# Causal masks, activation table calls, the order of calls and the first head of a two-layer attention kernel

## The reference, cut to what matters

```python
xn = layer_norm(_layernorm(x), gamma_in)
q, k, v = heads(xn @ Wq) * 64 ** -0.5, heads(xn @ Wk), heads(xn @ Wv)
sim = einsum('bhid,bhjd->bhij', q, k)
sim = where(causal_mask, -max, sim)            # triu(ones, k=1)
attn = softmax(sim)
out = einsum('bhij,bhjd->bhid', attn, v)
adj = clip(attn + eye(n), 0, 1); deg = sum(adj, -1)
feats = v
for l in range(2):
    h = feats @ gnn_w[l] + gnn_b[l]
    feats = gelu(adj @ h / deg + feats)        # per head
out = out + feats @ lin_w + lin_b
y = x + _layernorm(layer_norm(out @ Wo, gamma_out))
# then two layers of local attention and feed-forward, a norm and a residual
```

## Time and profile before

| What | Value |
|---|---|
| Median of 3 runs | 1573.04 us (1572.93 to 1578.7) |
| Profiled execution | 1574.63 us |
| Its span, first to last instruction | 1572.8 us |
| Mean granted TensorE clock | 0.975 |
| Busy: TensorE, weight load, VectorE, ScalarE, POOL | 92%, 71%, 75%, 63%, 23% |
| First product of the maxima of head 0 | 34.88 us |
| First scores of head 0 | 47.65 us |

### The profile page before, as it was taken

The page is one execution under the profiler, slowest core; times in us unless marked ns, Lnnn a source line. Parts: engine busy times, 40 slices in busy tenths (PEclk is TensorE's granted clock), DMA queues, the critical chain, the costliest instruction groups (busy, mean ns, idle before and its releaser), DMA issues. The chain is left out here.

```text
span 1572.8 us, 29162 instructions
## 1 busy us (share of the span) xinstructions
PE 1441.3 (92%) x10194; PEld 1109.0 (71%) x10194; DVE 1181.4 (75%) x3237; ACT 995.3 (63%) x2307; POOL 367.7 (23%) x474
## 2 busy tenths in 40 slices
PE   4899999999999999999999999999788999999896
PEld 3577877778777787777777777777455666666663
DVE  4577777777777777777878777776787888888875
ACT  2366666666666666666666666666355877778573
POOL 2022222221122111222222222223222332222211
PEclk8899999999999999999999999999987999999998
DMA  6021111211112111121111121220300000100100
GB/s 172 14 51 32 28 28 29 43 39 28 28 31 48 32 28 28 31 44 35 28 28 28 38 45 28 58 48 1 91 21 11 21 21 21 25 18 21 28 12 20
DMA packets 41147, 54.36 MB, mean 35 GB/s; under 512 B 11774, under 2 KB 23978, under 8 KB 41002
## 3 DMA queue, kind: packets, MB, share of 16 engines
q1 hardware_dynamic: 41002, 52.51, 15.0%
HBM read 9.89 MB, written 1.05 MB: 7 GB/s over the span
## 5 line engine op out<-in xcount | busy, mean ns | idle before, releaser
L1098 ACT ACTIVATE t<-PS 128x512 f32<-128x512 f32 (+3 forms) x384 | 188.9, 492 | 148.4 <-PE PS L661 94.5
L1544 DVE TENSOR_REDUCE t<-PS 128x1 f32<-128x512 f32 (+3 forms) x384 | 210.7, 550 | 77.3 <-PE PS L634 54.4
L1561 DVE TENSOR_TENSOR t<-t 128x512 fp32r<-128x512 f32 (+3 forms) x384 | 211.5, 551 | 9.6 <-ACT t L1099 9.4
L1099 ACT ACTIVATE t<-PS 128x512 fp32r<-128x512 f32 (+3 forms) x384 | 188.6, 491 | 0.0
L713 PE MATMUL PS<-t 128*128 128x512 f32 (+3 forms) x384 | 150.1, 391 | 21.9 <-ACT t L1132 21.6
L632 PE MATMUL PS<-t 128*128 128x512 f32 (+3 forms) x384 | 140.8, 391 | 24.8 <-DMA t<-t 13.0
L1248 ACT ACTIVATE t<-PS,t 128x128 f32<-128x128 f32 x256 | 113.2, 463 | 67.7 <-DVE t L1804 67.7
L660 PE MATMUL PS<-t 128*128 128x512 f32 (+3 forms) x384 | 149.0, 388 | 2.7 <-DMA t<-t 2.2
L1408 POOL TENSOR_TENSOR t<-t 128x16 f32<-128x16 f32 x32 | 92.8, 2900 | 234.1 <-DVE t L1666 234.1
L678 PE MATMUL PS<-t 128*66 128x512 f32 (+3 forms) x384 | 138.8, 361 | 0.0
L661 PE MATMUL PS<-t 65*128 65x512 f32 (+3 forms) x384 | 133.7, 348 | 0.0
(11 more groups left out here) (189 smaller groups left out, 3872.5 us busy)
## 6 DMA issues: line engine op xcount, KB each, us to landing
t<-t SPq DMA_DIRECT2D x188, 128.0 KB, 2.3
t<-t SPq DMA_DIRECT2D x64, 256.0 KB, 3.4
t<-in_c_rot SPq DMA_DIRECT2D x4, 512.0 KB, 5.6
t<-in_L_ffn_wqkv SPq DMA_DIRECT2D x2, 768.0 KB, 7.6
t<-in_L_attn_Wv SPq DMA_DIRECT2D x2, 512.0 KB, 7.4
out<-t SPq DMA_DIRECT2D x4, 256.0 KB, 2.3
t<-in_L_ffn_w SPq DMA_DIRECT2D x2, 341.0 KB
t<-in_L_attn_x SPq DMA_DIRECT2D x2, 256.0 KB, 3.2
```

Of the source, the lines that this page charges most:

```text
L1098: e.activation(Es[:, k % NS, 0:n], b[:, 0:n], ACT.Exp).then_inc(a_es.up((t, k)), 1)
L1099: e.activation(Eh[:, o:o + n], b[:, 0:n], ACT.Exp).then_inc(a_eh.up((t, k)), 1)
L1544: e.tensor_reduce(n[:, c, ib:ib + 1], bank(k % 2)[:, 0:hi - lo], AX.X, ALU.max, negate=True).then_inc(d_max.up((t, k)), 1)
L1561: e.tensor_tensor(El[:, o:o + n], Es[:, k % NS, 0:n], f32(Eh[:, o:o + n]), ALU.subtract).then_inc(d_el.up((t, k)), 1)
```

## The change

- **Masks.** The mask products (lines 634 and 663) and `cmB` are gone. VectorE adds the mask in place in PSUM on 128x128, `causal` ahead of a maximum and `acausal` ahead of an exponential, with new signals `d_cm` and `d_sm`. ScalarE's `scores` waits for `d_sm` in the diagonal tiles.
- **Tables.** Before all else ScalarE takes the exponential of one column into `fsc`. In each turn `exp_table` stands after tile 4 of the scores, and `gelu_table` after tile 11, one column each.
- **Order.** The calls of the loop are put in another order on TensorE, VectorE, ScalarE and POOL. `widen_v` is split off `widen`; both stand at the end of POOL's turn.
- **Head 0.** POOL writes the weights of K and of Q twice side by side (`twins`, in the space of `El`), so that `head0` on TensorE gives K in both halves of bank 2 + c and Q in both halves of bank 4 + c. ScalarE and VectorE write `K1`, `K2`, `Q1` and `Q2` of head 0 from there, without `part(0)` and `double(0)`. The work ahead of the loop is interleaved with the maxima of head 0, `part(1)` and `double(1)` come ahead of the loads of WG, Wo and the second half of x, and `mrow(0)` behind them. The loads of `wqkv0`, the band, the shift and `gam_out` move into turn 4.

```diff
             def smax(t, k):
...
-                diag = c == ib // 4
-                m = e.matmul(bank(b)[:, 0:hi - lo], Q1[r][:, ib * P:(ib + 1) * P], K1[r][:, lo:hi], start=True, stop=not diag)
-                if diag:
-                    m = e.matmul(bank(b)[:, hi - lo - P:hi - lo], identB[:], cmB[:, 0, :], start=False, stop=True)
-                m.then_inc(p_max.up((t, k)), 1)
+                e.matmul(bank(b)[:, 0:hi - lo], Q1[r][:, ib * P:(ib + 1) * P], K1[r][:, lo:hi], start=True,
+                         stop=True).then_inc(p_max.up((t, k)), 1)
...
-                if diag:
-                    m = e.matmul(b[:, 0:P], identB[:], cmB[:, 1, :], start=False, stop=True)
...
+            def causal(t, k):
...
+                q.wait_ge(*p_max[t, k])
+                s = bank(k % 2)[:, o:o + P]
+                e.tensor_tensor(s, s, cm[:, 0, :], ALU.add).then_inc(d_cm.up((t, k)), 1)
...
+            def acausal(t, k):
...
+                q.wait_ge(*p_sc[t, k])
+                s = bank(2 + k % 2)[:, 0:P]
+                e.tensor_tensor(s, s, cm[:, 1, :], ALU.add).then_inc(d_sm.up((t, k)), 1)
...
             def scores(t, k):                      # ScalarE
...
-                q.wait_ge(*p_sc[t, k])
                 q.wait_ge(*(d_el[t, k - NS] if k >= NS else d_el[t - 1, k + NTL - NS]))
                 q.wait_ge(*p_hop[t - 1, k])
+                q.wait_ge(*(d_sm if jb >= 4 * c else p_sc)[t, k])
...
+            def gelu_table(t):
...
+                e.activation(fsc[:, 0:1], half[:, 0:1], ACT.Gelu)
...
+            def head0(c):                          # TensorE
+                q.wait_ge(*d_turn[c])
+                q.wait_ge(*w_wd[0])
+                sl = slice(c * 512, (c + 1) * 512)
+                for i in range(2):
+                    b = bank(2 + 2 * i + c)
+                    e.matmul(b, twins[:, i, 0, :], xh[:, sl], start=True, stop=False)
+                    e.matmul(b, twins[:, i, 1, :], xh[:, sl], start=False, stop=False)
+                    m = e.matmul(b, twins[:, i, 0, :], xl[:, sl], start=False, stop=True)
+                m.then_inc(p_proj.up((0, c)), 1)
...
+            def head0(c):                          # ScalarE
...
+                e.copy(K1[0][:, sl], bank(2 + c)).then_inc(a_k0.up(c), 1)
+                e.activation(Q1[0][:, sl], bank(4 + c), ACT.Copy, scale=0.125)
+                e.activation(Q2[0][0:64, sl], bank(4 + c)[0:64, :], ACT.Copy, scale=0.125).then_inc(a_q0.up(c), 1)
...
+            def head0(c):                          # VectorE
...
+                e.tensor_tensor(K2[0][0:64, sl], bank(2 + c)[0:64, :], f32(K1[0][0:64, sl]), ALU.subtract)
+                q.wait_ge(*a_q0[c])
+                e.scalar_tensor_tensor(Q1[0][64:P, sl], bank(4 + c)[64:P, :], 0.125, f32(Q1[0][64:P, sl]), ALU.mult,
+                                       ALU.subtract).then_inc(d_low.up((0, c)), 1)
...
-            part(0)
-            double(0)
-            for t in range(NH):
+            part(1)
+            double(1)
...
+            mrow(0)
+            for t in range(1, NH):
```

More of the change, by code:

```diff
@@ L274, in program @@
         a_lin = signal("a_lin", range(1, 5))
-        a_hi = signal("a_hi", halves)
+        a_hi = signal("a_hi", halves[2:])
+        a_k0 = signal("a_k0", range(2))
+        a_q0 = signal("a_q0", range(2))
         a_v = signal("a_v", halves)
@@ L293, in program @@
         d_max = signal("d_max", maxes)
+        d_cm = signal("d_cm", maskings)
+        d_sm = signal("d_sm", [(t, k) for t, k in by_tile if tiles[k][1] >= 4 * tiles[k][0]])
         d_nm = signal("d_nm", heads)
@@ L778, in tensor @@
             turn(1, 1)
-            values()
-            for c in range(2):
-                proj(0, c, 2 + c)
-            for c in range(2):
-                proj(1, c, 4 + c)
-            for c in range(2):
-                projv(0, c)
-            for k in range(NTL):
+            head0(0)
+            head0(1)
+            values(0)
+            values(1)
+            proj(1, 0, 4)
+            proj(1, 1, 5)
+            smax(0, 0)
+            smax(0, 1)
+            mixed(0)
+            mixed(1)
+            smax(0, 2)
+            smax(0, 3)
+            projv(0, 0)
+            projv(0, 1)
+            for k in range(4, NTL):
                 smax(0, k)
@@ L815, in tensor @@
                     linear(2, 7)
+                scores(t, 5)
+                av(t, 1)
+                av(t, 2)
+                scores(t, 6)
+                graph2(t - 1, 10)
                 smax(t + 1, 4)
@@ L1160, in square @@
                 e.activation(sq, bank(QB, 2), ACT.Square).then_inc(a_sq.up(a), 1)
+            q.wait_ge(*w_half[0])
+            e.activation(fsc[:, 0:1], half[:, 0:1], ACT.Exp)
             turn(0)
             turn(1)
-            values()
-            for c in range(2):
-                proj(0, c, 2 + c)
-            for c in range(2):
-                proj(1, c, 4 + c)
-            for c in range(2):
-                projv(0, c)
+            head0(0)
+            head0(1)
+            values(0)
+            values(1)
+            proj(1, 0, 4)
+            proj(1, 1, 5)
+            mixed(0)
+            mixed(1)
+            projv(0, 0)
+            projv(0, 1)
             mrow(0)
@@ L1204, in scalar @@
                 scores(t, 11)
+                hopend(t - 1, 1)
+                gelu_table(t)
                 feats(t, 0)
@@ L1207, in scalar @@
                 share(t, 0)
+                av(t, 1)
                 proj(t + 2, 1, 3)
-                av(t, 1)
+                mrow(t + 1)
+                hopend(t, 0)
                 gelu2(t - 1)
@@ L1212, in scalar @@
                     square(0)
-                mrow(t + 1)
-                hopend(t, 0)
                 feats(t, 1)
@@ L1343, in widen @@
                     return
-                h = t % HA
-                D, R = WD[t % 2], WR[t % 2]
+                h, D = t % HA, WD[t % 2]
+                if t == 0:
+                    for i, (W, name) in enumerate(((WkD, "wk"), (WqD, "wq"))):
+                        q.wait_ge(ld[name], 16)
+                        src = W[:, 0:1, :].broadcast_to([P, 2, DH])
+                        hi, lo = [twins[:, i, s, :].rearrange("p (a d) -> p a d", a=2) for s in range(2)]
+                        e.tensor_copy(hi, src).then_inc(own.up(), 1)
+                        q.wait_ge(*own.now())
+                        m = e.tensor_tensor(lo, src, hi.bitcast(F32), ALU.subtract)
+                    m.then_inc(w_wd.up(t), 1)
+                    return
                 src = [W[:, h, :] for W in (WkD, WqD)]
```

256 lines of the change are left out of this document (155 added, 101 removed).

## The result

The changed kernel takes 1619.29 us (median of 4 runs, 1603.95 to 1625.46) against 1572.99: 2.6% slower, ratio 1.026 [1.022, 1.030]. The forecast was 1528, 3% faster.

The account below looks back on a forecast made before the run. TensorE was taken to bound the loop, busy 31.5 of 32.43 us a head. Loop 35 plus start 10 made 45 us off the profiled 1574.6, giving 1529.6, and 1528 for the median; 8-in-10 range 1490 to 1560.

Parts of the forecast that it names:

- the table load "already lies ahead of its wait": ScalarE, head's start: the exponential's table load starts before the score is there, so in-loop table calls bring nothing.
- ScalarE waits for TensorE anyway: ScalarE's scores: it already waits at most units and for its table, so waiting for on-time masks costs nothing.
- The masks on TensorE, 2.1 us a head: Main loop: removing sixteen mask products at 0.13 us each frees 2.1 us of TensorE a head, 66 us in all.
- The masks on VectorE, 0.20 each: Main loop: sixteen PSUM additions add 3.2 us a head, giving VectorE 27.4 us of work in heads without norms.
- The kept idle time, 3.1: VectorE, heads without norms: of 8.3 us idle a head, 3.1 stays, so VectorE alone could take 30.5 us.
- Heavy heads, 32.6: Twelve later heads with layer norms on VectorE: expected at 32.6 us each instead of 33.10.
- both signs in its last sentence: Loop: the forecast is wrong if ScalarE waits for masks at several units or the clock leaves 1.00 through TensorE pauses.
- The slower rival: VectorE's in-order queue: masks not ready block maxima and remainders, and TensorE waits for banks; 1611 us, chance 0.07.
- I cost the chain at nothing while VectorE is on time: Diagonal scores: the chain TensorE, VectorE, exponential costs nothing, or up to 0.3 us per mask where VectorE is late.
- The tables: ScalarE: in-loop table calls bring nothing; only the first load, 1.28 us long behind gamma's arrival, comes forward.
- The rival's figure, up to 82 us: ScalarE's loop: if both 1.28 us loads a head were exposed, table calls save up to 82 us; about 1450, chance 0.03.
- The start: Before the loop: first maximum at about 20 us, first scores at about 38; 10 us gained, a steadier clock only upside.

Follow-up runs that it names:

- b_last: The kernel before, with ScalarE's wait for the score in `scores` put last of the three waits: 1615.55 us, ratio 1.025.
- a_first: The changed kernel with one edit, ScalarE's wait for the score put first again in `scores`, masks still on VectorE: 1576.43 us, ratio 0.999.
- b_masks: The kernel before with only the masks changed: VectorE adds all sixteen a head, calls otherwise in the old order: 1689.64 us, ratio 1.072.
- a_notab: `a_pemasks` without the calls `exp_table` and `gelu_table` in ScalarE's loop: 1546.56 us, ratio 0.983.
- b_start: `a_pemasks` with the old call order and tables in the loop, so the kernel before with the new start alone: 1568.43 us, ratio 0.996.
- a_fill: `a_pemasks` with 39 idle TensorE products added among head 0's maxima, behind `mrow(0)` and in the first turn: 1538.17 us, ratio 0.977.
- a_pemasks: The changed kernel with the masks back on TensorE and ScalarE's wait for the score first: 1544.54 us, ratio 0.980.

## Why the prediction was wrong

**The step that failed: the table load "already lies ahead of its wait".** That was read from the kernel before and carried over, though the diff in `scores` moves the score's wait. The forecast used this row against the table calls and never asked what puts the load there. It also counted ScalarE's new wait at nothing because "ScalarE waits for TensorE anyway". That wait was the cover of the load: once the load stands behind it, every head pays for it. The runs gave 43 and 38 us, and 1.2 us a head at full clock in `b_last`.

**The masks on TensorE, 2.1 us a head: mis-sized.** The step of 0.13 came from two single places. Over whole heads, mask products add 1.25 us to TensorE's busy time, the lower bound of 0.08, and removing them shortens plain heads by 1.2 and heavy ones by 0.6: 25 us in the kernel instead of 66. The Trainium skill's figure (TensorE: Matmul & The Clock Gate, Back-to-back issue gap), about 81 ns and, as an estimate from it, 41 us in all, was set aside for the trace's dearer places. The 0.08 per mask of the whole heads agrees with it. The total is lower still: without the masks a plain head loses 1.25 us of work and only 0.97 of its length, so TensorE waits for part of what it saves.

**The masks on VectorE, 0.20 each: right in size.** 27.77 us of work against 27.4. **The kept idle time, 3.1: nearly right in plain heads.** Of 8.3 us of idle time the forecast's five rows name 6.8, and the other 1.5 was put at nothing without a reason. `a_first` has (95.27 - 83.82) / 3 = 3.8 in these three heads of 31.76 each, where 27.4 + 3.1 = 30.5 was worked out:

```profile
429.30:524.57 95.27, 89.97 (x578) 75.28 (x577) 83.82 (x259) 65.05 (x145) 21.03 (x36) 1.00 0.16 34
```

But the gain was counted from 32.43 as the masks' doing, and the new order with the masks still on TensorE brings plain heads to 31.91. The 31.89 of VectorE's masks is then no gain.

**Heavy heads, 32.6: wrong.** `a_first` has 34.44. The power on POOL was counted as 0.8 us of idle time on VectorE. In the place shown it holds up masks and maxima queued behind it, so that TensorE waits, and the clock of these heads is 0.95 instead of 1.00. The prediction named both signs in its last sentence (the clock leaving 1.00, ScalarE waiting for masks) and gave them no price.

**The slower rival** had the right sign and very nearly the right time (1611), through the wrong mechanism: its 1611 is luck. In-order blocking is real, 112 us in `b_masks` with the fall of the clock, but the new order takes most of it away; what made this kernel slower than before is the exposed load. "I cost the chain at nothing while VectorE is on time" fails with it.

**The tables.** That the calls bring nothing held (`a_notab`). The rival's figure, up to 82 us if both loads of a head were exposed, was of the right size for the wrong kernel: one of the two became exposed, by the change itself, and cost half of it.

**The start.** The first maxima came at 19.39 (20 forecast) and the first scores at 37.61 (38 forecast). The 10 us did not arrive: the first turn runs at half clock until shortly before 70 us, while before the window from 55 on was already at 1.00, and 6 to 8 us are left in `b_start`. The clock was weighed as an upside only; it took part of the gain, as `a_fill` shows.

## The faster version

`a_fill` beats both kernels: 1538.2 and, again, 1539.2, ratio 0.976 [0.973, 0.980]. It keeps the new order, the new start and the table calls, has the masks on TensorE and the score's wait first, and holds the clock in the start with 39 idle products.

## What to carry to other kernels

Where an activation needs a new table, look at which waits stand at the load and which at the activation, and see to it that the wait that ends last stands at the activation. In the four kernels compared here that was so where this wait was written first, and not where it was written last. Before work is moved off the engine with the highest busy share, price its removal by leaving it out altogether: here that bounds the gain at 25 us, and the 57 us which the work costs on the other engine decide. An engine at 80% with an in-order queue is no free room where its queue holds waits of its own.

## What the hardware showed

TensorE stayed at its lower clock, 1.2 GHz, through 25 us in which it was recorded as busy without a gap. In `a_pemasks` the clock fell in the window 30 to 35, after idle time of some 2 us in each window of five, and was at 0.50 from 35 to 65 us although TensorE was busy for 5.00 of 5.00 us in every window from 40 on:

```profile
25.00:30.00 5.00, 3.19 (x24) 2.62 (x23) 2.90 (x7) 1.30 (x4) 1.63 (x6) 1.00 0.58 115
30.00:35.00 5.00, 3.04 (x11) 1.51 (x11) 2.63 (x6) 0.26 (x1) 0.00 (x0) 0.63 0.67 162
35.00:40.00 5.00, 2.69 (x8) 1.69 (x8) 0.78 (x3) 1.59 (x4) 0.00 (x0) 0.50 0.21 59
40.00:45.00 5.00, 5.00 (x16) 2.84 (x16) 3.83 (x15) 1.36 (x5) 0.00 (x0) 0.50 0.00 0
```

In the kernel before it was at 0.54 in the window 50 to 55 and at 1.00 from 55 on, after TensorE had been busy for only 2.65 us of the window 45 to 50 and for 4.82 of the next. What decides when it comes back is open. So is why a pause of 1.2 to 1.3 us costs clock in some heads and not in others: the plain head of the kernel after shown above pauses for 1.23 us and has 1.00, its turns 2 to 5 have 0.94, and `b_last` pauses for 1.19 us in nearly every head and has 1.00 throughout the loop.

What a fall of the clock costs is plain, though. Another plain head of the kernel after, the same work at a mean clock of 0.95, takes 33.81 us instead of 32.71:

```profile
382.60:416.41 33.81, 31.55 (x194) 26.27 (x193) 27.79 (x87) 21.68 (x49) 7.01 (x12) 0.95 0.16 33
```

The recorded 0.23 us of a mask product says little about its cost, 0.08 of busy time over whole heads. The 0.29 us recorded for a mask in PSUM on VectorE is 0.20 of its queue (L1646 at 823.35 to L1634 at 823.55 in the rows above, 0.29 recorded).
